# Gathered means and scores: an earlier mean, an earlier sort, earlier gathers, and two slots moved from TensorE to VectorE

## The reference

```
retrieved = jnp.mean(item_embeddings[indices], axis=1)      # (512, 50) indices, rows of 512
fused_input = jnp.concatenate([user_rep, retrieved], axis=1)
fused_rep = fused_input @ W_fuse + b_fuse                   # (512, 1024) @ (1024, 512)
logits = fused_rep @ W_proj + b_proj                        # (512, 512) @ (512, 12500)
```

## Time and profile before

| | |
|---|---|
| median of three runs | 317.55 us |
| profiled execution | 315.62 us |
| its span | 313.8 us |
| TensorE busy | 300.0 us (96%) |
| VectorE busy | 246.6 us (79%) |
| ScalarE busy | 128.5 us (41%) |
| GpSimd busy | 75.6 us (24%) |
| mean granted TensorE clock | 0.993 |
| DMA | 75.13 MB, mean 239 GB/s |

### The profile page before, as it was taken

The page is one execution under the profiler, slowest core; times in us unless marked ns, Lnnn a source line. Parts: engine busy times, 40 slices in busy tenths (PEclk is TensorE's granted clock), DMA queues, the critical chain, the costliest instruction groups (busy, mean ns, idle before and its releaser), DMA issues.

```text
span 313.8 us, 4058 instructions
## 1 busy us (share of the span) xinstructions
PE 300.0 (96%) x1400; PEld 245.1 (78%) x1400; DVE 246.6 (79%) x369; ACT 128.5 (41%) x166; POOL 75.6 (24%) x76
## 2 busy tenths in 40 slices
PE   3999799999979999999999999999999999999995
PEld 1567678798859889888887888888888888888884
DVE  5888598948489863999869997979979798996123
ACT  2123565530002002417257555674656647563220
POOL 5777784538777700000000000000000000000000
PEclk9999799999999999999999999999999999999999
DMA  7999999797999521268728874939759295253315
GB/s 269 341 362 341 376 367 408 227 353 268 257 364 302 166 100 67 70 223 295 254 77 346 267 285 166 356 116 301 288 168 352 110 335 214 102 159 131 133 65 196
DMA packets 32547, 75.13 MB, mean 239 GB/s; under 512 B 4511, under 2 KB 20655, under 8 KB 32528
## 3 DMA queue, kind: packets, MB, share of 16 engines
q1 hardware_dynamic: 25264, 58.06, 52.0%
q0 software_dynamic: 5536, 13.73, 13.8%
q10 hardware_dynamic: 1728, 3.10, 2.6%
HBM read 52.85 MB, written 25.60 MB: 250 GB/s over the span
## 4 chain that ended last, share of the span: by engine, by line
PE 67%; DMA 3%; DVE 2%; issue 1%; SPq 1%; ACT 0%; DVEq 0%; ACTq 0%
PE pair L1127 18%; PE pair L1203 16%; PE pair L1205 16%; PE pair L1206 16%; DMA logits<-out_sb 3%; PE pair L1113 2%; SPq L350 1%; DVE out_sb L858 0%; DVE t_sums L903 0%; DVE early L905 0%; DVE w_lo L914 0%; PE pair L1103 0%; ACT odd_sum L607 0%; DVE pair L791 0%; DVE part_out L1068 0%
## 5 line engine op out<-in xcount | busy, mean ns | idle before, releaser
L442 POOL DMA_INDIRECT ring<-item_embeddings,rows x56 | 61.0, 1089 | 29.9 <-issue 13.1
L1127 PE MATMUL pair<-w_hi,f_hi 128*128 128x500 f32 x144 | 56.8, 394 | 2.0 <-DVE out_sb L858 1.5
L1127 PE MATMUL pair<-w_lo,f_hi 128*128 128x500 f32 x144 | 56.3, 391 | 0.0
L1127 PE MATMUL pair<-w_hi,f_lo 128*128 128x500 f32 x144 | 56.0, 389 | 0.0
L1203 PE MATMUL pair<-w_hi,s_hi 128*128 128x500 f32 x128 | 49.9, 390 | 0.6 <-ACT odd_sum L607 0.6
L1205 PE MATMUL pair<-w_lo,s_hi 128*128 128x500 f32 x128 | 49.9, 390 | 0.0
L1206 PE MATMUL pair<-w_hi,s_lo 128*128 128x500 f32 x128 | 49.8, 389 | 0.0
L791 DVE SCALAR_TENSOR_TENSOR pair<-ring,mask,pair 128x512 f32<-128x512 f32 x46 | 34.6, 753 | 6.5 <-DMA ring<-item_embeddings,rows 2.9
L1206 PE MATMUL pair<-w_hi,f_lo 128*128 128x500 f32 x96 | 37.2, 388 | 0.0
L1203 PE MATMUL pair<-w_hi,f_hi 128*128 128x500 f32 x96 | 37.2, 388 | 0.0
L1205 PE MATMUL pair<-w_lo,f_hi 128*128 128x500 f32 x96 | 37.2, 388 | 0.0
(11 more groups left out here) (139 smaller groups left out, 438.2 us busy)
## 6 DMA issues: line engine op xcount, KB each, us to landing
w_raw<-w_proj SPq DMA_DIRECT2D x26, 500.0 KB, 7.6
early<-w_proj SPq DMA_DIRECT2D x24, 500.0 KB, 6.6
logits<-part_out SPq DMA_DIRECT2D x21, 500.0 KB, 3.2
logits<-out_sb SPq DMA_DIRECT2D x28, 250.0 KB, 2.9
logits<-out_sb SPq DMA_DIRECT2D x10, 500.0 KB, 2.9
logits<-out_sb ACTq DMA_DIRECT2D x8, 250.0 KB, 6.8
early<-b_proj SPq DMA_DIRECT2D x8, 250.0 KB, 8.1
s_sum<-b_proj SPq DMA_DIRECT2D x8, 250.0 KB, 6.5
```

The source lines that it names most:

```text
L442: return nc.gpsimd.indirect_dma_start(out=to, out_offset=None, in_=table, in_offset=bass.IndirectOffsetOnAxis(ap=column, axis=0), **how)
L1127: m = nc.tensor.matmul(ps[:, 0:CHUNK], f[:, t, k, :], w, start=begin, stop=(f is f_lo and k == HK - 1))
```

## The change

- **ScalarE:** `mean(0)` goes ahead of the cast of chunk 2's first half.
- **VectorE, order:** `sort(2)` moves from the middle of tile 0's stage to the head of the kernel, right behind `sort(1)`. The adds of tile 1's slots and the splits are woven in another order.
- **Gathers:** tile 2 and 3 get their home gather ahead of slot 2 (before: 8) and their lap ahead of slot 7 (before: 13), and VectorE adds `home` after slot 6 (before: 12).
- **Slots of tile 1:** `PE_LAST` goes from 2 to 0: VectorE adds slots 9 and 10, TensorE takes the list alone. ScalarE's two masked identities (`keep_last`) fall away.
- **TensorE:** the list's four matmuls leave `turn_sum` for a new `turn_slots`, called ahead of tile 0's last chunk, with a semaphore of its own.

```diff
-HOME_AT = (2, 2, 8, 8)
-LAPS_AT = (8, 8, 13, 13)
+HOME_AT = (2, 2, 2, 2)
+LAPS_AT = (8, 8, 7, 7)
-PE_LAST = 2
+PE_LAST = 0
-HOME_AFTER = (0, 5, 12, 12)
+HOME_AFTER = (0, 5, 6, 6)
@@ place_free
                 elif j > last_add(u):
-                    pool.wait_ge(ret_turned, u + 1)
+                    pool.wait_ge(late_summed, j - last_add(u))
@@ scalar
-            split_hi(2, (0,))
             mean(0)
-            split_hi(2, (1,))
+            split_hi(2)
@@ vector
             sort(1)
+            sort(2)
             count_columns()
...
-            for i in range(4):
-                add(1, i)
+            add(1, 0)
+            add(1, 1)
+            split_lo(2, (0,))
             fused_lo(0, (0, 1))
-            split_lo(2, (0,))
+            add(1, 2)
             fused_lo(0, (2, 3))
             list_taken(1)
             split_lo(2, (1,))
+            add(1, 3)
             split_lo(3)
...
             split_lo(4)
-            sort(2)
             add_home(1)
...
-            add(1, 8)
+            for i in range(8, last_add(1) + 1):
+                add(1, i)
@@ tensor
+            def turn_slots():
+                wait_evacuated(pe, group_of(0, RESIDENT - 3))
+                for j in range(PE_LAST + 1):
+                    i = last_add(1) + 1 + j
+                    if j < PE_LAST:
+                        pe.wait_ge(kept_ready, PE_FIRST + j + 1)
+                    else:
+                        pe.wait_ge(list_kept, 2)
+                    pe.wait_ge(slot_landed[place(1, i)], 16 * slot_uses(1, i))
+                    sum_in(ring[:, place(1, i), :], ret_t[:, j, :], first=(j == 0), ps=turn_bank(1)).then_inc(late_summed, 1)
...
             for t in range(TILES):
                 for c in range(RESIDENT):
                     halfway = t + 1 if c == RESIDENT - 1 and t + 1 < TILES else None
+                    if halfway == 1:
+                        turn_slots()
                     project_resident(t, c, halfway)
```

More of the change, by code:

```diff
@@ L194, in retrieval_scores @@
         slot_summed = sem("slot_summed")
+        late_summed = sem("late_summed")
         user_fused = sem("user_fused")
@@ L1085, in sum_in @@
                 return m
+            def turn_slots():
[8 more added lines that the diff above has]
+                    sum_in(ring[:, place(1, i), :], ret_t[:, j, :], first=(j == 0), ps=turn_bank(1)).then_inc(late_summed, 1)
             def turn_sum(t):
-                wait_evacuated(pe, group_of(t - 1, RESIDENT - 3))
                 if t == 1:
[L1090 to L1097, removed]
                     pe.wait_ge(added, adds_done(1, last_add(1)))
@@ L1100, in turn_sum @@
                     return
+                wait_evacuated(pe, group_of(t - 1, RESIDENT - 3))
                 pe.wait_ge(added, adds_done(t, last_add(t)))
```

## The result

The changed kernel takes 315.17 us (median of 16 executions, 312.42 to 318.83), the kernel before on the same chip 316.59 us (16 executions, 315.27 to 319.05). The ratio is 0.9944, with a 95% interval of 0.9922 to 0.9966: faster by 0.56%. The forecast was 319.8 us and slower. The ratio leaves out three executions of the change (317.38 to 318.83 us) that count as slow; with all 16 the medians give 0.9955. The profiled execution took 313.39 us (before: 315.62), its span is 311.5 us (before: 313.8). It is the third fastest of the 16, so its gain of 2.2 us is larger than that of the medians, 1.4 us.

The account below looks back on a forecast made before the run. TensorE, busy 300.0 of 313.8 us, was taken to bound, with tile 2's turn waiting for tile 1's block 2 store. +0.8 (store) + 1.4 (clock) = +2.2 us gave a 319.8 us median, range 315.3 to 321.6.

Parts of the forecast that it names:

- Sort early: VectorE at the kernel's head: `sort(2)` takes 2.1 us, partly hidden by idling, so tile 0's sum ends 1.1 us later.
- Mean early: Turn to tile 0: `fuse(0)` starts 1.1 us earlier, first projection stays at 39.08, low clock moves to the projections; gain nothing.
- Tile 0's stage: TensorE loses two `sum_in` slots, gathers delay chunk 7 by 0.8 us; `fuse(1)` at 65.5 to 65.8, gain 1.4 us.
- VectorE and the turn's candidates: Tile 1's stage: `add_home(2)` eats the gain, block 0 evacuated at 76.0; lap wait goes, block 2's store (issued 82.0) binds.
- So the store lands about 1 us later: Tile 1's block 2 store competes with about seven full gathers; 0.8 us taken, bounds 1.5 us earlier to 2.5 later.
- the store comes early: Rival, chance 0.27: lap and its queue held the loads; store lands 1.5 to 2.5 us sooner, 313.9 to 316.5 us.
- The clock again: Turn to tile 2's sum: TensorE idles 4.4 us, so the clock falls over `turn_sum(2)` and `fuse(2)`, costing 1.4 us.
- `add_home(2)` ahead of block 0: VectorE in tile 1's stage: adds 1.3 us, so `fuse(1)` to block 0's evacuation takes 10.4 us, not 9.1.

Follow-up runs that it names:

- e10: The changed kernel with tile 0's mean back behind the cast of chunk 2's first half: 316.17 us, ratio 0.9958 to the kernel before.
- e11: The changed kernel with `sort(2)` back in tile 0's stage, behind `split_lo(4)`: 313.82 us, ratio 0.9904 to the kernel before.
- e1: The changed kernel run again unaltered on another chip: 315.36 us against 316.57 for the kernel before, ratio 0.9953.
- e2: The kernel before with only tile 2's home gather (ahead of slot 6, not 8) and lap (slot 10, not 13) issued earlier: 313.5 us, ratio 0.9882.
- e3: The changed kernel with tile 2's lap back next to the loads (ahead of slot 16, home added after slot 12): 314.14 us, ratio 0.9905 to the kernel before.
- e15: The changed kernel with the three tables for homes and laps as before: 314.44 us, ratio 0.9930 to the kernel before.
- e9: The changed kernel with SyncE's loads of tile 1's stage moved behind stores in tile 2's stage: 314.66 us, ratio 0.9930 to the kernel before.
- e12: The changed kernel with slots 9 and 10 of tile 1 back on TensorE (`PE_LAST` = 2): 318.29 us, ratio 1.0021 to the kernel before.
- e4: The kernel before with the loads of chunk 8 and the first round's blocks moved behind tile 2's stores 1 and 4: 314.62 us, ratio 0.9927.

## Why the prediction was wrong

- **Sort early: right, larger.** The sum ended at 32.53, not 32.1.
- **Mean early: right.** `fuse(0)` at 32.99 (forecast 32.55), the first projection at 39.06 (39.08), the low stretch on the projections. e10 confirms that the edit gains nothing. The Trainium skill ("TensorE: Matmul & The Clock Gate", section "Why this matters for your kernels") would have kept the clock there; against it stand 2.04 us of idling and 0.50 in the row of 40.30 to 43.60.
- **Tile 0's stage: right.** `turn_slots` at 61.13 (60.65 to 60.95), `fuse(1)` at 65.87 (65.5 to 65.8). The early sort costs here, since its gathers run beside chunk 7. I gave them 0.8 us and left them in the sum as if unavoidable; e11 measured 1.3 us at the end. What I did not price is the wait and the low clock at `turn_slots` that this brings in some executions. In e1 it waits 1.09 us, and `fuse(1)` at 67.20 has gained nothing on the 67.06 of before.
- **VectorE and the turn's candidates: right in place, off in one length.** Block 0 was evacuated at 76.25 (76.0), the lap's wait went, and the store took its place. Its issue came at 81.16, not 82.0, because the stall of SyncE at line 350 went too. I had taken that stall for fixed.
- **"So the store lands about 1 us later": the step that failed.** It landed 2.25 us earlier in the profile of the change, 0.84 from the issue and 1.41 from the transfer, and 0.35 us earlier in that of e1. When the gathers would be issued was right (78.38, forecast 78.3); what they cost the store was wrong on both sides. For the change I counted seven full gathers, 4.9 us. They moved 1.28 MB, as much as five of 0.26 MB, and took 3.5 us, since the ones issued last had not moved by the landing. For before I counted the lap, four nearly empty gathers and three full ones, 3.8 us. They took 5.5 us: 1.56 MB less the lap's 0.26 is 1.3 MB, again as much as five full ones, and the earlier trace rows had shown 1.11 MB of it in the last 4.4 us alone. So the full gathers weighed about the same in both kernels. What went away was the lap and some 300 small packets (882 packets before, 458 now, 128 of the difference the lap's), and with them the sign of the step.
- **What the rivals had.** The landing lay past my lower bound, 1.5 us earlier, but in my rival "the store comes early" (chance 0.27, 313.9 to 316.5 us, measured 315.17). Its reason, that the lap and its queue held the loads, is borne out by e2; e3 shows that the lap alone is not enough. The round robin of the Trainium skill ("DMA: Bandwidth & Descriptors", section "Queues, rings and completion order"), as I had applied it, made every gather from 78.3 on hold the store. The trace does not contradict it; it shows that a gather takes no turns before its packets move, 5.6 us after its issue here.
- **The clock again: it fell with the store.** TensorE waits 0.90 us at the turn instead of 4.4 in the profiled execution, and the 1.4 us that the sum has for the clock are 0. In e1 it waits 1.48 us, and no low stretch follows. Nine of the 28 executions of the change show a mean clock of 0.989 (median 317.07 us, longer than the kernel before). Among the profiles, e15 has that mean clock: its `turn_slots` stood idle 2.84 us and a long low stretch followed. So a further loss by the clock exists, in a third of the executions, but not where I had put it: in the profiles of e9, e10, e12 and e15 a low stretch stands at `turn_slots`, and no profile has one at the turn. None of the nine themselves was profiled, so that this is its place there too is likely, not shown.
- **`add_home(2)` ahead of block 0: right.** From `fuse(1)` to the evacuation of block 0 it took 10.38 us, forecast 10.4, and so it eats the gain of `fuse(1)`. Unforeseen was that ScalarE waits 1.87 us for tile 0's last stores ahead of `fused_hi(1)` (the row below), but this costs nothing: e1 has no such wait and takes 10.38 us too, and e15, which has no `add_home(2)` there, takes 9.07.

```profile
67.37 0.57 ACT L535 COPY out_sb<-pair 128x500 f32<-128x500 f32 x1 [1.87 <-DMA logits<-out_sb]
```

Where the gain comes from is shown in parts. The tables alone give 0.9956 and all the rest alone 0.993; together 0.9944. These three intervals overlap, so none of them can be called the best. If the parts added, the whole would be near 0.989; the noise nearly covers the difference. Either part takes the lap away from the loads, and that is worth something once, which would explain it. That the change gains less than e2 because it brings tile 3's gathers forward into the loads fits the books of the two (1.28 MB of gathers against 0.62), and so do e11's 1.3 us for the early sort; no run parts the two. Nor is it shown what makes the landings differ from one execution to the next.

## What to carry to other kernels

Where two queues share the DMA engines, price the other queue by the engine time of the packets that move between an issue and its landing, read from the profile, small packets and accumulating ones included, not by the DMAs issued. A load that nobody needs yet, written ahead of stores in one queue, sets those stores: moving it needs no estimate of sharing (e4; in the changed kernel, e9, its gain is within the noise). And change one such table at a time: a small edit of two numbers (e2) gave twice what the whole change gives. Last, one profile of each kernel is one draw of several: the two of this change put the same store's landing 1.9 us apart.

## What had not been expected of the hardware

- The first 5 us of loads after a pause move slowly: 1.37 MB in 5 us with the queue of loads at 88.7% (274 GB/s), against 410 GB/s in the stretch of 89.80 to 91.00.
- The lap's packets, which add to what is there, cost twice as much for a byte. In e4 the lap was alone from 80.5 to 81.5 us: 93 packets of 2 KB, 0.177 us of an engine for each (1.030 x 16 us / 93). In the change from 84.5 to 85 us a packet of the full gathers, 4 KB, took 0.178 us (0.444 x 8 us / 20).

```profile
q0 software_dynamic: 93, 0.19, 103.0%
```
```profile
q0 software_dynamic: 20, 0.08, 44.4%
```

- The clock followed TensorE's idle gaps more neatly than the two gaps of before could tell. Of the gaps over 0.8 us between 20 and 100 us in the profiles of before, the change, e1 to e4 and e9 to e15, ten were of 2.00 to 2.87 us, and each was followed by a stretch at 0.50; thirteen were of 0.90 to 1.94 us, and none was. It is no sharp rule: nearer the head, a gap of 1.87 us in e3 was followed by one too. But at such a place some tenths of a microsecond in a load's landing decide over about 1.4 us. Two rows, of e2 (no low stretch behind it) and of e1 (one behind it):

```profile
39.47 0.47 PE L1127 MATMUL pair<-w_hi,f_hi 128*128 128x500 f32 x1 [1.94 <-DVE f_lo L841]
```
```profile
39.07 0.46 PE L1134 MATMUL pair<-w_hi,f_hi 128*128 128x500 f32 x1 [2.00 <-DVE f_lo L841]
```
